# An adapter with layer norm over 128 batches: h in pairs, b1 from TensorE, language numbers loaded two at a time

## The chip, the cores and the metric

One core of a Trainium2 chip runs the whole program. The metric is the device time of one execution in microseconds (us). PE is TensorE, PEld its weight loads, DVE is VectorE, ACT is ScalarE, POOL is GpSimd and SP the queue that issues most DMAs. A q behind a name (PEldq, ACTq) marks what the engine's sequencer does itself: register loads, branches, DMA issues.

## The reference

For each of 128 batches, with x[b] of 128 rows by 512 and a language number lang in 0 to 9:

```python
h = relu(x[b] @ W1[lang] + b1[lang])          # 128 x 128
y = x[b] + h @ W2[lang] + b2[lang]            # 128 x 512
n = (y - mean(y)) / sqrt(var(y) + 1e-5)
out[b] = x[b] + n * gamma[lang] + beta[lang]
```

## The kernel before

Batches go through in order, 16 to a turn: turn 0 is unrolled, turns 1 to 6 are one hardware loop (`all_turns`), and turn 7 is unrolled. Each engine has its own program, and semaphores that count batches tie them together. x lies in 16 slots of `x_io`; SP moves it in pairs of batches (512 KB), stores a pair once it is finished, and one pair later loads that slot with the x of the next turn (`store_pair`, `load_pair`, L217 to L226).

For batch t the work goes as follows.
- PE turns x by four transposes (`turn_x`, L385) into a bank `ps_T`. ACT copies it to `x_T` (L323).
- PE multiplies by W1 in full fp32 (`first_product`, L392: four products, shown as eight weight loads and matmuls) into `ps_h`. ACT copies h to `h_rows` (L328), PE turns it (`turn_h`, L400), and ACT applies relu with b1 as its per-partition bias, twice: into `h_high`, a rounded fp32r (L337), and into `h_T`, fp32 (L338). The bias is picked by a language number in a register of ACT. POOL subtracts the two to get `h_low` (L263).
- PE forms y in one of four banks `ps_y` (`second_product`): b2 by a bf16 product with `pick` and `parts` (L409), then h_high by w2_high (L411), h_high by w2_low (L412), h_low by w2_high (L414). For slots 1, 5, 9 and 13 there is no L409: POOL adds b2 to x (L279), and `x_b2` takes the place of x.
- DVE adds x and takes the row sum (`add_x`, L501), ACT squares (L343), DVE takes the mean of a pair (L506), ACT the root of a pair (L348), DVE the reciprocal (L511), then y minus mean times gamma (`scale`, L518) and the end result into the slot of x (`finish`, L526). POOL adds beta to x for it (L272).

In PE's program step j of a turn holds turn_h(t-1), turn_x(t+1), first_product(t) and second_product(t-3). A second product waits until its bank is free, that is until `finish` of four batches earlier. DVE runs norms four batches behind.

Language numbers stand in `lang_ids` and are needed in registers. At the start of each turn PE, ACT, POOL and DVE each load those of the whole turn and of the batches that lag behind, with one TENSOR_LOAD in the trace (`langs_of`, L139): 20 values on PE, 16 on ACT, 20 on POOL and 16 on DVE in a turn of the loop. Behind the last turn PE and ACT load one, POOL two and DVE four.

Ahead of turn 0, gamma and beta are spread over the partitions by PE (L452, from `parts`, which SP fills with three bf16 pieces of each row), and DVE cuts w2 into high and low parts in five chunks (L488, L490), from a buffer `w2_all` of its own. PE does first products of batches 0 to 4 meanwhile and then waits for the last chunk (L436). SP's order there is x pair 0, w1, `parts`, x pair 1, w2 with x pairs 2 and 3 in between, x pairs 4 to 7, and b2 for all partitions (L215).

Of the kernel before, what the change touches and what calls it, by code (L numbers as in the profile page):

```python
# [13 lines left out]
UNROLL = 16  # L14
PAIRS = UNROLL // 2
Y_BANKS = 4
LAG = 4
H_SLOTS = 8
H_T_SLOTS = 4
B2_BY_POOL = (1, 5, 9, 13)  # L20
B2_LATE = 2
NORM_LAG = 4


def build(nc, x, ids, w1, b1, w2, b2, gamma, beta, out):
# [3 lines left out]
    TURNS = B // UNROLL  # L29
    W_CHUNKS = 5  # L30
    LC = L // W_CHUNKS
    X_AFTER_W2 = (1, 4)
    assert S == 128 and A == 128 and H == 512 and B % UNROLL == 0 and TURNS > 2

# [4 lines left out]
    with ExitStack() as ctx:  # L39
# [9 lines left out]

        w1_all = sb("w1_all", [128, L, C, A], F32)  # L50
        w2_all = sb("w2_all", [128, L, H], F32)
# [6 lines left out]
        b1_all = sb("b1_all", [128, L], F32)  # L58

# [4 lines left out]
        parts = sb("parts", [128, H], BF16)  # L64
        pick_row = sb("pick_row", [128, 3 * L], BF16)
# [6 lines left out]

        x_io = sb("x_io", [128, UNROLL, H], F32)
        x_T = sb("x_T", [128, 2, C, S], F32)
        h_rows = sb("h_rows", [128, 2, A], F32)
        h_T = sb("h_T", [128, H_T_SLOTS, S], F32)
        h_high = sb("h_high", [128, H_SLOTS, S], F32R)
        h_low = sb("h_low", [128, H_SLOTS, S], F32R)
        squares = cut
        row_sum = sb("row_sum", [128, UNROLL], F32)  # L80
        mean = sb("mean", [128, UNROLL], F32)
        sq_sum = sb("sq_sum", [128, UNROLL], F32)
        table_load = sb("table_load", [128, 1], F32)
        std = sb("std", [128, UNROLL], F32)
        rstd = sb("rstd", [128, UNROLL], F32)
# [7 lines left out]
        s_b1 = sem("s_b1")  # L93
        s_rows = sem("s_rows")
        s_b2 = sem("s_b2")
        x_b2_ready = sem("x_b2_ready")
# [11 lines left out]
        pick_ready = sem("pick_ready")  # L108
        cut_step = sem("cut_step")
        parts_ready = sem("parts_ready")  # L110
# [4 lines left out]
        x_beta_ready = sem("x_beta_ready")  # L115
        x_turned = sem("x_turned")
        x_T_ready = sem("x_T_ready")
        h_summed = sem("h_summed")
# [5 lines left out]
        adapted = sem("adapted")  # L124
        y_ready = sem("y_ready")
        squared = sem("squared")
        scaled = sem("scaled")
        out_ready = sem("out_ready")

# [7 lines left out]
        def langs_of(engine, t, n):  # L137

            return nc.values_load_multi_w_load_instructions(  # L139
                lang_ids[0:1, bass.ds(t, n)], engines=[engine.engine], min_val=0, max_val=L - 1,  # L140
                skip_runtime_bounds_check_because="VectorE keeps lang_ids within the tables")[1]

        def seconds_done(j, first, last):

            if j < 0:
                return 0 if first else j - LAG + 1
            if first:
                return max(0, j - LAG + 1)
            if last:
                return min(j, j - LAG + 1 + (j + 1) // (UNROLL // (LAG - 1)))  # L150
            return j - LAG + 1

        def seconds(j, first, last):

            return range(seconds_done(j - 1, first, last), seconds_done(j, first, last))

        LEFT = B - seconds_done(UNROLL - 1, False, True) - (TURNS - 1) * UNROLL
        LEFT_NORMS = B - seconds_done(UNROLL - 2, False, True) - (TURNS - 1) * UNROLL

# [3 lines left out]
        def b2_by_pool(j, first):  # L163
            return j in B2_BY_POOL[B2_LATE if first else 0:]

# [3 lines left out]
        def b2_count(i, j):  # L169

            return i * len(B2_BY_POOL) + B2_BY_POOL.index(j) + 1 - B2_LATE

        def w2_chunk(table, n):
            return table[:, n * LC:(n + 1) * LC, :]

# [4 lines left out]

# [6 lines left out]
        def _(sp):  # L187
            sp.dma_start(ids_raw[:, :], ids.rearrange("(a b) -> a b", a=1)).then_inc(s_ids, 16)
            for k, table in enumerate((b2, gamma, beta)):
                sp.dma_start(rows[k * L:(k + 1) * L, :], table).then_inc(s_rows, 16)  # L190
            def first_x(k):
                sp.dma_start(x_io[:, 2 * k:2 * k + 2, :], x_pairs[:, k, :, :]).then_inc(x_loaded[k], 16)

            def load_w2(n):
                sp.dma_start(w2_chunk(w2_all, n), w2[n * LC:(n + 1) * LC].rearrange("l a h -> a l h"))\
# [13 lines left out]
            for n in range(W_CHUNKS):  # L209
                load_w2(n)  # L210
                if n in X_AFTER_W2:
                    first_x(2 + X_AFTER_W2.index(n))
            for k in range(2 + len(X_AFTER_W2), PAIRS):
                first_x(k)
            sp.dma_start(b2_all[:, :, :], b2.partition_broadcast(128)).then_inc(s_b2, 16)  # L215

            def store_pair(i, k):  # L217
                sp.wait_ge(out_ready, i * UNROLL + 2 * k + 2)
# [9 lines left out]

            def turn(i, first, last):
                for k in range(PAIRS):  # L230
                    if last and k == PAIRS - 1:
                        for b in range(2):
                            sp.wait_ge(out_ready, B - 1 + b)
                            sp.dma_start(out[B - 2 + b], x_io[:, UNROLL - 2 + b, :]).then_inc(stored[k], 16)
# [12 lines left out]
        def _(pool):  # L247
            nc.gpsimd.memset(parts[:, :], 0.0).then_inc(parts_zero, 1)
            nc.gpsimd.memset(identity[:, :], 0.0).then_inc(set_ready, 1)
# [9 lines left out]
            def low_h(t, j):  # L259
                pool.wait_ge(h_high_ready, t + 1)  # L260
                pool.wait_ge(h_T_ready, t + 1)

                nc.gpsimd.tensor_tensor(h_low[:, j % H_SLOTS, :], h_T[:, j % H_T_SLOTS, :],  # L263
                                        h_high[:, j % H_SLOTS, :].bitcast(F32), ALU.subtract).then_inc(h_low_ready, 1)

            pool.wait_ge(ids_ready, 1)
            pool.wait_ge(spread_act, L)
# [314 lines left out]
```

## Time and profile before

| | |
|---|---|
| median of 3 runs | 377.81 us (376.56 to 378.6) |
| profiled execution, span | 373.9 us |
| PE busy | 317.1 us (85%) |
| DVE busy | 314.1 us (84%) |
| ACT busy | 284.8 us (76%) |
| POOL busy | 257.4 us (69%) |
| mean granted TensorE clock | 0.972 |
| DMA over the span | 202 GB/s |

The profiled execution is one of its own; the profile gives its span, from the first to the last instruction, as its only time, and the median of the timed runs lies 3.9 us above that. Busy shares are averages over stages. Ends of matmuls are modelled, so that the distance between starts of consecutive matmuls tells their cost, not the duration beside them. Some matmul records are missing.

### The profile page before, as it was taken

The page shows a single profiled execution, that of the slowest core. Times are in us where ns is not written, and L with a number is a line of the kernel's source. Part 1 is how long each engine was busy: PE and PEld are TensorE (multiplying, and loading weights), DVE is VectorE, ACT ScalarE, POOL GpSimd, SP SyncE. Part 2 cuts the span into 40 slices and gives each one's busy share as a digit, 9 for nine tenths or more (in the row PEclk, how much of TensorE's full clock was granted, in tenths as well). Part 3 has the DMA queues.
Part 4 walks back from the last instruction along what each step waited for, and adds up shares of the span by engine and source line. Part 5 has one row for each costly group of instructions (what it writes and reads, how often), then busy time and mean ns, then how long its engine had stood idle before and what let it go on. Part 6 is the DMA issues. An engine that isn't in the chain of part 4 may idle for free. (4 is left out here: it accounts for less than half of the span.)

```text
span 373.9 us, 9114 instructions
## 1 busy us (share of the span) xinstructions
PE 317.1 (85%) x2133; PEld 274.5 (73%) x2167; DVE 314.1 (84%) x669; ACT 284.8 (76%) x848; POOL 257.4 (69%) x299
## 2 busy tenths in 40 slices
PE   1888996999878996899879997989969999879870
PEld 0277985889767995789768895879858897767850
DVE  3695995799869995699957997699957998799997
ACT  5666994799687995789858895979947996967871
POOL 2034784688677884788847885878846886767882
PEclk9999998999999999899989999999989999999996
DMA  7999365376744666366634766447653666556333
GB/s 179 320 387 419 118 222 175 113 236 228 231 148 173 224 224 224 112 203 240 218 125 168 234 227 224 156 155 232 227 172 112 231 224 229 178 183 213 124 122 130
DMA packets 43047, 75.35 MB, mean 202 GB/s; under 512 B 3612, under 2 KB 8823, under 8 KB 42901
## 3 DMA queue, kind: packets, MB, share of 16 engines
q1 hardware_dynamic: 41733, 75.14, 58.8%
q10 hardware_dynamic: 1296, 0.01, 0.2%
q8 instruction: 8, 0.13, 0.2%
q14 instruction: 10, 0.08, 0.1%
HBM read 41.49 MB, written 33.55 MB: 201 GB/s over the span
## 5 line engine op out<-in xcount | busy, mean ns | idle before, releaser
L272 POOL TENSOR_TENSOR x_io<-x_io,beta_all 128x512 f32<-128x512 f32 x128 | 163.7, 1279 | 15.1 <-DVE ps_y L501 13.8
L392 PE MATMUL ps_h<-w_all,x_T 128*128 x1024 | 138.0, 278 | 0.4 <-ACT x_T L323 0.4
L392 PEld LDWEIGHTS ps_h<-w_all,x_T 128*128 128x128 f32 x1024 | 126.8, 195 | 0.8 <-issue 0.7
L263 POOL TENSOR_TENSOR h_low<-h_T,h_high 128x128 fp32r<-128x128 f32 x128 | 60.3, 471 | 94.5 <-ACT h_T L338 87.2
L343 ACT ACTIVATE cut<-ps_y,row_sum 128x512 bf16<-128x512 f32 x128 | 88.8, 694 | 15.7 <-DVE ps_y L501 15.7
L526 DVE SCALAR_TENSOR_TENSOR x_io<-ps_y,rstd,x_io 128x512 f32<-128x512 f32 x128 | 94.6, 739 | 0.0
L518 DVE SCALAR_TENSOR_TENSOR ps_y<-ps_y,mean,gamma_all 128x512 f32<-128x512 f32 x128 | 89.6, 744 | 0.7
L501 DVE SCALAR_TENSOR_TENSOR ps_y<-ps_y,x_io 128x512 f32<-128x512 f32 x98 | 67.4, 688 | 20.4 <-PE ps_y L414 20.4
L385 PE MATMUL ps_T<-identity,x_io 128*128 128x128 f32 x512 | 78.7, 277 | 6.1 <-DMA x_io<-in_x 6.1
L337 ACT ACTIVATE h_high<-ps_hT,b_all 128x128 fp32r<-128x128 f32 x128 | 46.2, 361 | 44.9 <-PE ps_y L414 29.6
L411 PE MATMUL ps_y<-w_high,h_high 128*128 x128 | 71.3, 557 | 7.7 <-DVE x_io L526 4.6
L323 ACT COPY x_T<-ps_T 128x512 f32<-128x512 f32 x128 | 74.8, 585 | 0.0
L385 PEld LDWEIGHTS ps_T<-identity,x_io 128*128 128x128 f32 x512 | 61.3, 143 | 15.0 <-issue 6.6
L400 PE MATMUL ps_hT<-identity,h_rows 128*128 128x128 f32 x128 | 36.4, 284 | 21.7 <-ACT h_rows L328 14.4
L412 PE MATMUL ps_y<-w_low,h_high 128*128 x128 | 51.6, 403 | 0.0
L414 PE MATMUL ps_y<-w_high,h_low 128*128 x128 | 51.4, 402 | 0.0
L338 ACT ACTIVATE h_T<-ps_hT,b_all 128x128 f32<-128x128 f32 x128 | 46.0, 359 | 0.0
L400 PEld LDWEIGHTS ps_hT<-identity,h_rows 128*128 128x128 f32 x128 | 18.2, 142 | 35.5 <-ACT h_rows L328 19.5
L328 ACT COPY h_rows<-ps_h 128x128 f32<-128x128 f32 x128 | 34.3, 268 | 12.7 <-PE ps_h L392 3.1
L506 DVE TENSOR_SCALAR mean<-row_sum 128x2 f32<-128x2 f32 x64 | 42.9, 670 | 0.0
L279 POOL TENSOR_TENSOR x_b<-x_io,b_all 128x512 f32<-128x512 f32 x30 | 38.5, 1285 | 0.0
L409 PE MATMUL ps_y<-parts,pick 128*128 128x512 bf16 x65 | 24.7, 380 | 8.1 <-DVE x_io L526 7.9
(43 smaller groups left out, 219.5 us busy)
## 6 DMA issues: line engine op xcount, KB each, us to landing
x_io<-in_x SPq DMA_DIRECT2D x64, 512.0 KB, 4.1
out<-x_io SPq DMA_DIRECT2D x63, 512.0 KB, 3.0
w_all<-in_L_cond_W SPq DMA_DIRECT2D x10, 512.0 KB, 6.8
b_all<-in_L_cond_b SPq DMA_DIRECT2D x1, 2560.0 KB, 17.2
out<-x_io SPq DMA_DIRECT2D x2, 256.0 KB, 2.0
parts<-cut SPq DMA_DIRECT2D x3, 30.0 KB, 3.6
rows<-in_L_cond_b SPq DMA_DIRECT2D x1, 20.0 KB
rows<-in_L_cond_gamma SPq DMA_DIRECT2D x1, 20.0 KB
```

The costliest lines, as they stand in the source:

```text
L263: nc.gpsimd.tensor_tensor(h_low[:, j % H_SLOTS, :], h_T[:, j % H_T_SLOTS, :], h_high[:, j % H_SLOTS, :].bitcast(F32), ALU.subtract).then_i ...
L272: nc.gpsimd.tensor_tensor(x_io[:, j, :], x_io[:, j, :], of_lang(beta_all, lang), ALU.add)\
L323: nc.scalar.copy(x_T[:, j % 2, :, :], ps_T[j % 2][:, :, :]).then_inc(x_T_ready, 1)
L343: nc.scalar.activation(squares[:, j % 2, :], ps_y[j % Y_BANKS][:, :], ACT.Square, scale=-float(H), bias=row_sum[:, j:j + 1], accum_out=sq_ ...
L385: last = nc.tensor.transpose(ps_T[j % 2][:, c, :], x_io[:, j, c * 128:(c + 1) * 128], identity[:, :])
L392: last = nc.tensor.matmul(ps_h[:, 0:A], x_T[:, j % 2, c, :], w1_all[:, bass.ds(lang, 1), c, :].rearrange("p o a -> p (o a)"), start=(c == ...
L400: nc.tensor.transpose(ps_hT[:, 0:S], h_rows[:, j % 2, :], identity[:, :]).then_inc(h_turned, 1)
L411: nc.tensor.matmul(bank, h_high[:, h, :], of_lang(w2_high, lang), start=not with_b2, stop=False)
L412: nc.tensor.matmul(bank, h_high[:, h, :], of_lang(w2_low, lang), start=False, stop=False)
L501: nc.vector.scalar_tensor_tensor(bank, bank, 1.0, x_rows, ALU.mult, ALU.add, accum_out=row_sum[:, j:j + 1]).then_inc(y_ready, 1)
L518: nc.vector.scalar_tensor_tensor(bank, bank, mean[:, j:j + 1], of_lang(gamma_all, lang), ALU.subtract, ALU.mult).then_inc(scaled, 1)
L526: nc.vector.scalar_tensor_tensor(x_io[:, j, :], ps_y[j % Y_BANKS][:, :], rstd[:, j:j + 1], x_io[:, j, :], ALU.mult, ALU.add).then_inc(out_ ...
```

## The change

- **Pairs.** h is handled by pairs of batches: both first products write halves of the one bank `ps_h`, one ACT instruction of 256 columns copies both, both are turned into halves of `ps_hT`, and each split (high, T, low) is one instruction of 256 columns. Steps on every engine are pairs; 64 steps take the place of 128.
- **b1 by PE.** `first_product` begins with a bf16 product of `pick` and `b1_parts` (128 columns). relu moves to the copy of h ahead of the turn. ACT needs no language number any more. `b1_parts` is made as `parts` is: a load on ACT's queue, three casts and two subtractions on DVE, three DMAs on SP ahead of those of `parts`, one more memset on POOL.
- **Languages by two.** `langs_of` loads two values: PE twice in each step (for its first and its second products), DVE once, POOL once, and once more in the steps with an add of b2.
- **Order.** PE's step k: turn_x of pair k+1 and first products of pair k, interleaved; second products of pair k-2; turn_h of pair k. DVE's step: scales of pair k-3, adds of pair k-2, reciprocal and finishes of pair k-3. ACT's: the two copies of x_T interleaved with the two squares of pair k-3, copy of h, mean and root, then the split of h. POOL's: low part of pair k-1, beta for pair k-3, b2 for pair k-2 where it has one. The last step does two second pairs.
- **Mean on ACT**, after the copy of h, in place of L506 on DVE.
- **w2 staged in x_io.** `w2_all` is gone; the five chunks land in the slots of x pairs 3 to 7, and those pairs are loaded one by one when `w2_low_ready` tells that the chunk is cut. b2 for all partitions is issued behind them.
- POOL's adds of b2 are now those of slots 4, 7, 10 and 13.

```diff
-UNROLL = 16
-LAG = 4
-B2_BY_POOL = (1, 5, 9, 13)
-NORM_LAG = 4
+SLOTS = 16
+LAG = 2
+NORM_LAG = LAG + 1
+H_PAIRS = 4
+B2_BY_POOL = (4, 7, 10, 13)
...
-        def langs_of(engine, t, n):
+        def langs_of(engine, t):
             return nc.values_load_multi_w_load_instructions(
-                lang_ids[0:1, bass.ds(t, n)], ...
+                lang_ids[0:1, bass.ds(t, 2)], ...
...
# SP
                 if n == 1:
-                    sp.wait_ge(parts_zero, 1)
+                    sp.wait_ge(parts_zero, 2)
+                    for k in range(3):
+                        sp.wait_ge(b1_cut_step, 2 * k + 1)
+                        sp.dma_start(b1_parts[32 * k:32 * k + L, :], b1_cut[:, k, :]).then_inc(b1_parts_ready, 16)
...
-                if n in X_AFTER_W2:
-                    first_x(2 + X_AFTER_W2.index(n))
-            for k in range(2 + len(X_AFTER_W2), PAIRS):
-                first_x(k)
+                if n == 1:
+                    first_x(2)
+            for n in range(W_CHUNKS):
+                sp.wait_ge(w2_low_ready, n + 1)
+                first_x(X_FIRST + n)
...
# POOL
+            def step(i, k, has_low, has_sum, has_norm, first):
+                if has_norm:
+                    langs = langs_of(pool, t - 2 * NORM_LAG)
+                if has_low:
+                    low_h(p - 1, (k - 1) % PAIRS)
+                if has_norm:
+                    for b in range(2):
+                        add_beta(t - 2 * NORM_LAG + b, (2 * (k - NORM_LAG) + b) % SLOTS, langs[b])
+                if has_sum:
+                    for b in range(2):
+                        j = (2 * (k - LAG) + b) % SLOTS
+                        if b2_by_pool(j, in_first):
+                            add_b2(t - 2 * LAG + b, j, langs_of(pool, t - 2 * LAG)[b], first)
...
# ACT
+            def copy_h(p, k):
+                act.wait_ge(h_summed, p + 1)
+                nc.scalar.activation(h_rows[:, k % 2, :, :].rearrange("p b a -> p (b a)"), ps_h[:, 0:2 * A], ACT.Relu)\
+                    .then_inc(h_rows_ready, 1)
+            def split_h(p, k, fresh):
+                act.wait_ge(h_turned, p + 1)
+                if not (fresh and k < H_PAIRS):
+                    act.wait_ge(adapted, 2 * (p - H_PAIRS) + 2)
+                if not (fresh and k < 2):
+                    act.wait_ge(h_low_ready, p - 1)
+                nc.scalar.copy(h_high[...], ps_hT[:, 0:2 * S]).then_inc(h_high_ready, 1)
+                nc.scalar.copy(h_T[...], ps_hT[:, 0:2 * S]).then_inc(h_T_ready, 1)
...
+            def mean_and_root(t, j):
+                nc.scalar.mul(mean[:, j:j + 2], row_sum[:, j:j + 2], 1.0 / H).then_inc(mean_ready, 1)
+                act.wait_ge(squared, t + 2)
+                nc.scalar.activation(std[:, j:j + 2], sq_sum[:, j:j + 2], ACT.Sqrt, ...).then_inc(std_ready, 1)
+            def step(i, k, has_x, has_h, has_norm, first):
+                for b in range(2):
+                    if has_x:
+                        act.wait_ge(x_turned, t + 3 + b)
+                        nc.scalar.copy(x_T[:, j % 4, :, :], ps_T[j % 2][:, :, :]).then_inc(x_T_ready, 1)
+                    if has_norm:
+                        square(u + b, v + b)
+                if has_h:
+                    copy_h(p, k)
+                if has_norm:
+                    mean_and_root(u, v)
+                if has_h:
+                    split_h(p, k, first)
...
# PE
+            def first_product(j, lang):
+                part = ps_h[:, (j % 2) * A:(j % 2 + 1) * A]
+                nc.tensor.matmul(part, of_lang(pick, lang), b1_parts[:, :], start=True, stop=False)
+                for c in range(C):
+                    last = nc.tensor.matmul(part, x_T[:, j % 4, c, :], ..., start=False, stop=(c == C - 1))
+                if j % 2 == 1:
+                    last.then_inc(h_summed, 1)
...
             def turn(i, first, last):
+                for k in range(PAIRS):
+                    langs = langs_of(pe, t)
+                    for b in range(2):
+                        pe.wait_ge(x_T_ready, t + b + 1)
+                        if not (last and k == PAIRS - 1):
+                            turn_x(i + (k + 1) // PAIRS, (2 * k + 2 + b) % SLOTS)
+                        first_product(2 * k + b, langs[b])
...
+                    for q in seconds(k, last):
+                        if not (first and q < 0):
+                            second_pair(i, q, first and 2 * q < Y_BANKS, first)
+                    turn_h(p, k)
...
# DVE
+            def step(i, k, sums, late_sums, has_norm, first):
+                if has_norm:
+                    langs = langs_of(dve, u)
+                    for b in range(2):
+                        scale(u + b, q, j + b, langs[b])
+                for s in sums:
+                    add_pair(i, s, first)
+                if has_norm:
+                    invert(q, j)
+                    for b in range(2):
+                        finish(u + b, q, j + b)
+                for s in late_sums:
+                    add_pair(i, s, first)
```

`second_pair` loads its two languages first, then is `second_product` for each batch of the pair, with the waits for `h_high` and `h_low` once a pair.

## Rows read from the trace of the kernel before

**Rows 1.** One line (L182), PE's branch at each loop end: times in ns, first and last.

```profile
L182 PEldq COMPARE_BRANCH  x6: 83/215/242, 97.7 to 312.7; - x6
```

**Rows 2.** Timeline of PE across a turn's end: start, us, what, [idle before].

```profile
134.78 0.40 PE L414 MATMUL ps_y<-w_high,h_low 128*128 x1
...
136.93 0.40 PE L414 MATMUL ps_y<-w_high,h_low 128*128 x1
...
139.29 0.39 PE L414 MATMUL ps_y<-w_high,h_low 128*128 x1
...
139.63 0.60 PE L385 MATMUL ps_T<-identity,x_io 128*128 128x128 f32 x4
140.06 1.06 PE L392 MATMUL ps_h<-w_all,x_T 128*128 x8
140.96 0.38 PE L409 MATMUL ps_y<-parts,pick 128*128 128x512 bf16 x1
...
143.09 0.32 PE L400 MATMUL ps_hT<-identity,h_rows 128*128 128x128 f32 x1 [1.05 <-issue]
...
147.69 0.33 PE L400 MATMUL ps_hT<-identity,h_rows 128*128 128x128 f32 x1 [2.03 <-ACT h_rows L328]
```

**Rows 3.** Waits by pair of lines: us in total, times, longest.

```profile
ACT h_high L337 <- PE ps_y L414: 29.6, 7, 4.4
```

**Rows 4.** Timeline of ACT in the same stretch.

```profile
146.37 0.37 ACT L337 ACTIVATE h_high<-ps_hT,b_all 128x128 fp32r<-128x128 f32 x1 [4.27 <-PE ps_y L414]
...
146.88 0.58 ACT L323 COPY x_T<-ps_T 128x512 f32<-128x512 f32 x1
147.35 0.29 ACT L328 COPY h_rows<-ps_h 128x128 f32<-128x128 f32 x1
147.51 0.72 ACT L343 ACTIVATE cut<-ps_y,row_sum 128x512 bf16<-128x512 f32 x1
```

**Rows 5.** One line (L139), the language loads: ns min/median/max, first and last start.

```profile
L139 ACTq TENSOR_LOAD <-lang_ids x9: 281/4657/4733, 2.9 to 362.9; - x9
L139 PEldq TENSOR_LOAD <-lang_ids x9: 310/2362/2504, 6.2 to 361.9; - x9
L139 POOLq TENSOR_LOAD <-lang_ids x9: 819/5857/6273, 19.2 to 364.1; - x9
L139 DVEq TENSOR_LOAD <-lang_ids x9: 350/1626/2226, 27.9 to 362.6; - x9
```

**Rows 6.** Instructions grouped by line: mean ns of one, idle time before them.

```profile
L506 DVE TENSOR_SCALAR mean<-row_sum 128x2 f32<-128x2 f32 x64 | 42.9, 670 | 0.0
...
L409 PEld LDWEIGHTS ps_y<-parts,pick 128*128 x98 | 9.7, 99 | 17.8 <-issue 17.7
```

**Rows 7.** Timeline of DVE in the same stretch.

```profile
140.66 1.39 DVE L518 SCALAR_TENSOR_TENSOR ps_y<-ps_y,mean,gamma_all 128x512 f32<-128x512 f32 x2
141.97 0.73 DVE L526 SCALAR_TENSOR_TENSOR x_io<-ps_y,rstd,x_io 128x512 f32<-128x512 f32 x1
142.62 0.68 DVE L501 SCALAR_TENSOR_TENSOR ps_y<-ps_y,x_io 128x512 f32<-128x512 f32 x1
```

**Rows 8.** Timeline of POOL: the same stretch, then the end.

```profile
139.98 1.28 POOL L272 TENSOR_TENSOR x_io<-x_io,beta_all 128x512 f32<-128x512 f32 x1
141.21 0.47 POOL L263 TENSOR_TENSOR h_low<-h_T,h_high 128x128 fp32r<-128x128 f32 x1
...
365.11 1.27 POOL L272 TENSOR_TENSOR x_io<-x_io,beta_all 128x512 f32<-128x512 f32 x1 [0.52 <-issue]
```

**Rows 9.** Timeline of the start: the first second product.

```profile
29.65 0.49 PE L411 MATMUL ps_y<-w_high,h_high 128*128 x1 [2.33 <-DVE w_low L490]
```

**Rows 10.** One line (L224), SP's loads of x.

```profile
DMA to landing us min/median/max: 3.7/4.1/5.4
```

**Rows 11.** Timeline of the end: the last L414 and the last finishes.

```profile
364.64 0.50 PE L414 MATMUL ps_y<-w_high,h_low 128*128 x1
...
369.89 1.41 DVE L526 SCALAR_TENSOR_TENSOR x_io<-ps_y,rstd,x_io 128x512 f32<-128x512 f32 x2
```

More of the change, by code:

```diff
@@ L373, in _ @@
+            for j in range(2):
+                act.wait_ge(x_turned, j + 1)
+                nc.scalar.copy(x_T[:, j, :, :], ps_T[j][:, :, :]).then_inc(x_T_ready, 1)
+            def turn(i, first, last):
+                for k in range(PAIRS):
+                    step(i, k, not (last and k == PAIRS - 1), True, not (first and k < NORM_LAG), first)
             all_turns(act, turn)
-            relu(B - 1, UNROLL - 1, langs_of(act, B - 1, 1)[0], False)
-            for k in range(LEFT_NORMS, 0, -1):
-                norm_sums(B - k, UNROLL - k)
+            for k in range(NORM_LAG):
+                step(TURNS, k, False, False, True, False)
@@ L419, in turn @@
-            def turn(i, first, last):
-                behind = 0 if first else LAG
-                langs = first_langs if first else langs_of(pe, i * UNROLL - behind, UNROLL + behind)
-                for j in range(UNROLL):
-                    t = i * UNROLL + j
-                    early = first and j <= LAG
-                    if not early:
-                        turn_h(t - 1, (j - 1) % UNROLL)
-                    if not (last and j == UNROLL - 1):
-                        turn_x(t + 1, i + (j + 1) // UNROLL, (j + 1) % UNROLL)
-                    if early and j > 0:
-                        turn_h(t - 1, (j - 1) % UNROLL)
-                    first_product(t, j, langs[j + behind])
-                    if first and j == LAG:
+                                            start=False, stop=(c == C - 1))
@@ L547, in step @@
-                if has_sum:
-                    add_x(t - 1, i + (j - 1) // UNROLL, (j - 1) % UNROLL, early)
-            def turn(i, first, last):
-                behind = 0 if first else NORM_LAG
-                langs = langs_of(dve, i * UNROLL - behind, UNROLL - NORM_LAG + behind)
-                for j in range(UNROLL):
-                    has_norm = not (first and j < NORM_LAG)
-                    step(i, j, langs[j - NORM_LAG + behind:] if has_norm else None, has_norm,
-                         not (first and j < 2), not (first and j == 0), first)
+                    langs = langs_of(dve, u)
@@ new lines, in step @@
+                    for b in range(2):
+                        scale(u + b, q, j + b, langs[b])
[3 more added lines that the diff above has]
+                    invert(q, j)
+                    for b in range(2):
+                        finish(u + b, q, j + b)
+                for s in late_sums:
+                    add_pair(i, s, first)
+            def turn(i, first, last):
+                for k in range(PAIRS):
+                    sums = [q for q in seconds(k, last) if not (first and q < 0)]
+                    step(i, k, sums[:1], sums[1:], not (first and k < NORM_LAG), first)
```

304 lines of the change are left out of this document (124 added, 180 removed).

## The prediction, made before the change was run

> **What bounds the kernel now.** I read busy shares first: PE and DVE both near 85%, which says little. So I measured a turn. PE's loop branch comes six times from 97.7 to 312.7 us, so a turn of 16 batches takes 43.0 us [rows 1], 5.38 a pair. The timeline of PE then shows what a batch costs when nothing waits: starts of L414 are 2.15 us apart without L409 and 2.36 with it [rows 2]; twelve batches in sixteen have it, so the mean is 2.31 and a turn of pure PE work 36.9. Inside a turn PE sets the pace; 6.1 us a turn are lost at its end. There PE waits 1.05 us for nothing that shows and 2.03 for h_rows [rows 2], ACT stands 4.27 us before L337 [rows 4], and so it is seven times, 29.6 us in all [rows 3]. The releaser named there, L414, had long been done: what holds ACT is its language load, 16 values in 4.66 us, while PE loads 20 in 2.36 and POOL 20 in 5.86 [rows 5]. The start up to 29.65 us [rows 9] and the end behind the last L414 at 364.64 [rows 11] are no steady work.
>
> **Language loads.** ACT's go altogether, and with them the chain that makes the turn's end expensive: up to 6.1 us a turn, 7 turns' ends, 43 us. In their place PE loads two values twice in a step. One value took PE 310 ns and twenty 2362 [rows 5]: 0.2 plus 0.108 a value, so two are 0.42 us. Such a load stalls PE only by what PE's queue has not covered. At the turn's end a load of 2.36 left 1.05 of idle PE [rows 2, 5], so 1.3 us of matmuls were queued ahead. I take the 0.42 as hidden, under the first products for the one and, for the one at the step's start, under second products queued before; this needs h_rows early, as worked out below. Bounds: 0 and 0.84 us a step. On DVE four values took 0.35 [rows 5]; I charge 0.25 a step, partly covered by the finish before it. On POOL two take 0.82, of which 0.52 showed as idle [rows 5, 8].
> The Trainium skill (Perfetto Trace Analysis, Sequencer Loop) says that a sequencer pushes engine instructions into a queue and runs control work itself. Only row 5 beside row 2 prices that here; the trace agrees in kind, with 1.3 us of cover.
>
> **PE.** b1 adds 128 bf16 products of 128 columns. No row has one. From below, a quarter of the 0.21 that L409's 512 columns add [rows 2] is 0.05; from above, a bf16 weight load is 0.10 [rows 6] and the moving side may not hide it. The neighbours are short too, one f32 transpose each 0.11 (four in 0.43 [rows 2]), so I take the upper end, 0.10. Batch 2.41, pair 4.82 us. The rest of PE's work is the same matmuls.
> TensorE: Matmul & The Clock Gate (the Trainium skill, Back-to-back issue gap) gives about 81 ns for a sustained load and matmul of 128 columns. By that the pair is 4.78 and the end 2.4 us earlier. The rows with 0.10 are nearer to this sequence.
>
> **ACT.** From starts: copy of x_T 0.47, square with its accumulator read 0.75 (the row has 0.72 for the square alone), copy of h 0.16 [rows 4]. From 128 to 512 columns a copy grows from 0.16 to 0.47, so 0.10 for each 128: copy of a pair 0.27, each split 0.36. Mean and root are small, 0.2 each. Sum 0.94 + 1.5 + 0.27 + 0.4 + 0.72 = 3.8 a step: not the bound.
>
> **DVE.** Two scales 1.31, one finish 0.65 [rows 7]; an add about the same. Six of them and a reciprocal: 4.0, with the load 4.25. L506 goes (0.67 each [rows 6]; for two numbers in a row that is mostly waiting); I book no gain, because DVE inside a turn waited for PE.
>
> **POOL.** low_h of 256 columns: 0.47 at 128, 1.28 at 512 [rows 8], so 0.74. Two betas at 1.23 from start to start, 2.46. Half an add of b2, 0.6. With loads of 0.5 each, 1.5 of them: 4.6 a step on average, but 5.4 in a step with b2.
>
> **The loops.** Three engines near 4.8 need their handoffs checked. Count from the end of PE's turn_h. ACT: handoff 0.3, split 0.72, copy 0.47, square 0.75, copy 0.47, square 0.75, copy of h 0.27, mean 0.3: DVE's scales start at 4.0, and the copy of h is there by 3.8, before PE wants it at 4.6. DVE: two scales, two adds, reciprocal, first finish end at 4.0 + 1.3 + 1.3 + 0.1 + 0.7 = 7.4; PE wants that bank in its next step at 4.82 + 2.86 = 7.7. Slack 0.3. The shorter loop, from scales to the next scales: 1.3, first add and handoff 0.75, then on ACT 0.75 + 0.47 + 0.75 + 0.27 + 0.3 = 4.6. Slack 0.2. POOL's b2: low_h starts at 1.2 and ends at 1.9, betas to 4.4, then up to 0.5 of load and 1.23: ready 5.6 to 6.2, and DVE's adds come at 5.3 (slots 4, 10) or 6.0 (7, 13). Late by 0 to 0.9 in four steps of a turn, part of it taken by the slack: I take 1.0 a turn, 0.13 a step. Step 4.95 us.
>
> **Ahead of the loop.** PE's second products began at 29.65, released by the last w2 chunk on DVE [rows 9]. The b1 path adds five small DVE instructions, which run while the rows for L472 are still coming, and three DMAs of SP ahead of those of `parts`. Each lands in some us but they overlap; the delay of `parts` is their issue, 0 to 1.5 us, I take 0.6. The memset on POOL is hidden by the same wait. Slots of x 3 to 7 wait for their chunks, some 2 us apart, the last near 30: landing takes 4.1, at most 5.4 [rows 10], and pair 7 is turned four steps later. Not on the path, and b2 behind it on SP's queue is first wanted some five steps on. The first products of three pairs fit before 30.3, as those of five batches did before 29.65. Later in the kernel, by the loop times above, pair k is finished 3.3 us into step k+4; SP loads its slot behind the store of pair k+1, 3.3 + 0.4 into step k+5, and the x lands 4.1 later, 3.0 into step k+6. PE turns it from the start of step k+7: slack 1.8 us, and 0.5 with a landing of 5.4. Free.
>
> **Sum.** 30.3; rest of that step (second pair 1.75, turn_h 0.22) 2.0; 61 steps of 4.95, 302; the extra second pair of the last step 1.75. DVE then has its late pair of adds (1.3, from 1.3 after PE's step), the norms of three pairs at 2.8 and one more pair of adds (1.3): 12.4 in all. 348.4, and 2.6 from the end of DVE (369.89 + 1.41 = 371.3 [rows 11]) to the end of the span, 373.9: span 351.0. The median lies 3.9 above the profiled span before; with that 354.9, so **355**.
>
> **Rivals.**
> 1. *Loads exposed on PE, slower than before.* Every step PE's queue is empty when a load starts, because it had just waited for h_rows or for a bank. Then 0.84 a step come on top: 61 x 0.84 = 51, 406 us; only one of two exposed gives 381. It decides from a step of 5.32 on (355 + 61 x 0.37 = 377.8). Against it: 1.3 us of cover [rows 2, 5] and h_rows 0.8 early. For it: all engines have 0.2 to 0.3 of slack, and a queue that waits is an empty one. Chance 0.11.
> 2. *The loops bind.* Each handoff 0.1 longer over four of them, or POOL late at each b2: step 5.15 to 5.3, 367 to 376. Chance 0.22.
> 3. *PE alone binds.* b1 at 0.05 to 0.10, POOL's lateness absorbed: step 4.72 to 4.82, 341 to 347. Chance 0.2.
> 4. *The turn's end stays.* If its 6.1 us are the branch or fetched code and not loads, 355 + 7 x 6 = 397. Against it: PE has the idle also where an unrolled turn begins without a branch, seven waits for six branches [rows 1, 3]. Chance 0.03.
> The forecast itself, step 4.87 to 5.1, has 0.44.
>
> **The numbers.** The range 341 to 377 holds rivals 2 and 3 and the forecast; 1 and 4 stay outside. A measurement of this kernel tells about 0.5% from no change. Faster by more: forecast, 2, 3, most of it: 0.85. Same: 0.04. Slower: 0.11, from 1 and 4.
>
> **What would show it.** A turn of 8 steps in about 39.6 us (43.0 before); L337's waits of 4 us gone; the granted clock at its upper level through the loop; PE with at most 0.2 us of idle a step; waits of DVE for x_b in steps of slots 4 and 10. Wrong: PE idle "issue" before first transposes or L409 in each step (rival 1), h_rows or finish as PE's releaser above 0.3 us a step (rival 2), gaps each 40 us (rival 4).

## The result and the profile after

The median of the changed kernel is 391.13 us (four runs, 389.4 to 393.35), that of the kernel before in the same session 377.69 (376.56 to 378.6). The ratio is 1.035 with a 95% interval of 1.031 to 1.040: the change made the kernel 3.5% slower. 355 was predicted, in a range of 341 to 377, and the slower side had 0.11. The profiled execution has a span of 391.3 us; 351.0 was worked out for it.

First the page of the changed kernel, its busy shares:

```profile
span 391.3 us, 9509 instructions
...
PE 333.6 (85%) x2294; PEld 279.3 (71%) x2295; DVE 287.6 (73%) x610; ACT 249.7 (64%) x719; POOL 244.4 (62%) x236
```

PE's share is what it was, DVE's fell from near 85% to 73%. So no engine took PE's place as the bound, and PE itself has holes. PE's branch at the loop's end (now L173), the counterpart of [rows 1], dates the turns:

```profile
L173 PEldq COMPARE_BRANCH  x6: 83/218/249, 101.0 to 319.8; - x6
```

A turn takes 43.8 us where it took 43.0. The first branch comes 3.3 us later than before, the last 7.1 later, and from there to the end of the span it is 71.5 us instead of 61.2. So the 17.4 us of difference between the two spans are 3.3 ahead of the first branch, 3.8 over five turns and 10.3 behind the last branch. The turn should have fallen to 39.6, and its end was indeed repaired: no wait of ACT for an L414 is left in the list of waits. What stands in its place (us in total, times, longest):

```profile
DVE ps_y L512 <- ACT mean L340: 75.5, 60, 3.1
PEld ps_T L381 <- issue: 43.1, 58, 5.5
...
PE ps_T L381 <- issue: 24.2, 54, 0.8
PE ps_y L411 <- DVE x_io L524: 12.0, 2, 8.6
...
DVE ps_y L500 <- POOL x_b L272: 7.3, 3, 6.1
```

The line to read is the third: 54 times, before the first transpose of a step, PE stands still and no semaphore holds it. (PEld is PE's weight load; its line is the same wait.) DVE's wait in the first line is DVE being early: in the fastest version below it is still 49.2 us in 60 waits. The timeline of PE shows two ends of steps in the unrolled turn 0 and two in the loop (start, us, what, idle before):

```profile
38.30 0.38 PE L397 MATMUL ps_hT<-identity,h_rows 128*128 128x128 f32 x2
38.52 0.60 PE L381 MATMUL ps_T<-identity,x_io 128*128 128x128 f32 x4
...
43.24 0.38 PE L397 MATMUL ps_hT<-identity,h_rows 128*128 128x128 f32 x2
...
156.51 0.38 PE L397 MATMUL ps_hT<-identity,h_rows 128*128 128x128 f32 x2
157.33 0.63 PE L381 MATMUL ps_T<-identity,x_io 128*128 128x128 f32 x4 [0.44 <-issue]
...
162.09 0.38 PE L397 MATMUL ps_hT<-identity,h_rows 128*128 128x128 f32 x2
```

From one turn_h to the next it is 4.94 us in turn 0, and there the transposes follow 0.22 behind it. In the loop it is 5.58, and they follow 0.82 behind it. From turn_h at 33.37 to turn_h at 358.49 lie 60 steps, so the mean is 5.42. What PE runs at that point between the two is its language load (L139; ns min/median/max of all, then single loads in two narrow stretches):

```profile
L139 PEldq TENSOR_LOAD <-lang_ids x128: 531/552/1639, 17.9 to 367.4; - x128
L139 POOLq TENSOR_LOAD <-lang_ids x94: 503/512/727, 28.1 to 376.2; - x94
L139 DVEq TENSOR_LOAD <-lang_ids x64: 523/528/784, 33.6 to 384.6; - x64
...
L139 PEldq TENSOR_LOAD <-lang_ids x1: 1522/1522/1522, 155.6 to 155.6; - x1
...
L139 PEldq TENSOR_LOAD <-lang_ids x1: 550/550/550, 158.8 to 158.8; - x1
```

The median says 0.55 us and hides the matter. 56 of the 128 loads take over 0.9 us (0.93 to 1.64, 50 of them 1.2 or more), and all 56 are loads at the start of a step; those in the middle of a step are all short. The load of 155.6 ends at 157.1, 0.3 before the transpose that comes late. And SP's queue at that time:

```profile
154.55 0.38 SPq L215 DMA_DIRECT2D out<-x_io  x1
155.12 0.39 SPq L220 DMA_DIRECT2D x_io<-in_x  x1
160.00 0.38 SPq L215 DMA_DIRECT2D out<-x_io  x1
160.57 0.39 SPq L220 DMA_DIRECT2D x_io<-in_x  x1
```

SP issues a store and a load of x each step, and the second issue ends at 155.5, where PE's long load begins. Each of the 56 long loads begins between 0.3 us ahead of and 0.7 us behind the end of an issue of SP. That is a coincidence until a run moves one of the two. It is also no rule: nine loads, of the start, of turn 0 and of the end, begin as close to an issue and take 0.53 to 0.83 us.

The end of the kernel (PE, then POOL and DVE):

```profile
358.49 0.38 PE L397 MATMUL ps_hT<-identity,h_rows 128*128 128x128 f32 x2
...
366.59 0.60 PE L411 MATMUL ps_y<-parts,pick 128*128 128x512 bf16 x1 [3.42 <-DVE x_io L524]
...
369.55 0.45 PE L397 MATMUL ps_hT<-identity,h_rows 128*128 128x128 f32 x2
...
373.95 1.26 POOL L272 TENSOR_TENSOR x_b<-x_io,b_all 128x512 f32<-128x512 f32 x1
375.33 0.70 DVE L500 SCALAR_TENSOR_TENSOR ps_y<-ps_y,x_b 128x512 f32<-128x512 f32 x1 [6.06 <-POOL x_b L272]
...
387.34 1.41 DVE L524 SCALAR_TENSOR_TENSOR x_io<-ps_y,rstd,x_io 128x512 f32<-128x512 f32 x2
```

The last step has two second pairs, and the later one needs a bank that DVE must finish first: 3.42 us of idle PE ahead of it, and only behind it comes the last turn_h. On that ACT and POOL's low_h depend; POOL's betas and x_b stand behind low_h in its program, and for x_b DVE waits 6.06 us. From turn_h of 358.49 to the end of the span it is 32.6 us (counted from its end at 358.7); the sum had 21.7. After the idle stretches the granted clock falls too: 1.00 through the loop, 0.57 from 366 us on, mostly the lower level of 1.2 GHz.

### The profile page after: what moved, and what is told of

It reads as the page before. It is cut to its first block and busy times, and to the rows that moved or that the text cites. A ratio compares the mean times of both kernels' runs of the same rounds, so it can differ in the third digit from the quotient of the medians.

```text
span 391.3 us, 9509 instructions
## 1 busy us (share of the span) xinstructions
PE 333.6 (85%) x2294; PEld 279.3 (71%) x2295; DVE 287.6 (73%) x610; ACT 249.7 (64%) x719; POOL 244.4 (62%) x236
## 5 line engine op out<-in xcount | busy, mean ns | idle before, releaser
L388 PE MATMUL ps_h<-w_all,x_T 128*128 x1024 | 142.0, 282 | 0.0
L259 POOL TENSOR_TENSOR h_low<-h_T,h_high 128x256 fp32r<-128x256 f32 x64 | 46.8, 731 | 134.5 <-ACT h_T L331 134.5
L524 DVE SCALAR_TENSOR_TENSOR x_io<-ps_y,rstd,x_io 128x512 f32<-128x512 f32 x128 | 90.2, 746 | 2.6
L329 ACT CAST h_high<-ps_hT 128x256 fp32r<-128x256 f32 x64 | 23.9, 373 | 86.5 <-PE ps_hT L397 86.5
L414 PE MATMUL ps_y<-w_high,h_high 128*128 x128 | 71.4, 558 | 0.1
L415 PE MATMUL ps_y<-w_low,h_high 128*128 x128 | 51.6, 404 | 0.0
L418 PE MATMUL ps_y<-w_high,h_low 128*128 x128 | 51.3, 401 | 0.0
L411 PE MATMUL ps_y<-parts,pick 128*128 128x512 bf16 x98 | 38.4, 391 | 12.1 <-DVE x_io L524 12.0
L272 POOL TENSOR_TENSOR x_b<-x_io,b_all 128x512 f32<-128x512 f32 x30 | 38.6, 1287 | 0.0
L418 PEld LDWEIGHTS ps_y<-w_high,h_low 128*128 128x128 f32 x128 | 24.6, 192 | 5.9
L411 PEld LDWEIGHTS ps_y<-parts,pick 128*128 x98 | 9.6, 98 | 26.6 <-issue 26.6
L386 PE MATMUL ps_h<-b_parts,pick 128*128 128x128 bf16 x128 | 28.0, 219 | 0.1
L415 PEld LDWEIGHTS ps_y<-w_low,h_high 128*128 128x128 f32 x128 | 24.9, 195 | 3.2
L500 DVE SCALAR_TENSOR_TENSOR ps_y<-ps_y,x_b 128x512 f32<-128x512 f32 x30 | 21.3, 710 | 7.4 <-POOL x_b L272 7.3
```

The lines of the kernel that those rows point to most:

```text
L388: last = nc.tensor.matmul(part, x_T[:, j % 4, c, :], w1_all[:, bass.ds(lang, 1), c, :].rearrange("p o a -> p (o a)"), start=False, stop=(c ...
L411: nc.tensor.matmul(bank, of_lang(pick, langs[b]), parts[:, :], start=True, stop=False)
L414: nc.tensor.matmul(bank, h_high[:, h, b, :], of_lang(w2_high, langs[b]), start=not with_b2, stop=False)
L415: nc.tensor.matmul(bank, h_high[:, h, b, :], of_lang(w2_low, langs[b]), start=False, stop=False)
L418: nc.tensor.matmul(bank, h_low[:, h, b, :], of_lang(w2_high, langs[b]), start=False, stop=True)\
L500: nc.vector.scalar_tensor_tensor(bank, bank, 1.0, x_rows, ALU.mult, ALU.add, accum_out=row_sum[:, j:j + 1]).then_inc(y_ready, 1)
```

## The experiments

The theory after reading: the load at a step's start is exposed on PE, since it stands where PE's sequencer has just waited for h_rows; and it is so long because SP issues DMAs at that moment. Rivals: the loops through ACT, DVE and POOL bind, so that PE's idle time is only where their wait shows (rival 2); the new matmul is what costs.

### The load taken ahead of the second products

```diff
-                    langs = langs_of(pe, t)
+                    langs = langs_of(pe, t) if k == 0 else next_langs
...
+                    if k < PAIRS - 1:
+                        next_langs = langs_of(pe, t + 2)
                     for q in seconds(k, last):
```

> After the change, with the language load at the start of PE's steps 1 to 7 of a turn moved ahead of the second products of the step before (two loads stand there together; step 0 of each turn keeps its load at the start). Theory (the load at the step's start is what holds PE: it takes 1.2 to 1.6 us where the other takes 0.54, and PE idles about 0.6 us a step for it): 52 of 60 steps lose 0.5 to 0.6 us, so 391 goes to 360 to 366, steps without the load at 4.8 to 4.95 as in turn 0. Rival (the loops over DVE and ACT set 5.4 us a step, and the load only fills a gap that is there anyway): 389 to 392, with DVE or ACT named as what PE waits for. Second rival (any load behind another is slow too, so that it is late for b2's product): about 375.

370.56 us, ratio 0.984 to the kernel before (0.979 to 0.989). That is 20.6 less than the changed kernel by the medians, and 23.1 by the spans of the profiled executions (368.2 and 391.3). PE's branches and loads:

```profile
L173 PEldq COMPARE_BRANCH  x6: 76/210/246, 98.2 to 300.8; - x6
...
L139 PEldq TENSOR_LOAD <-lang_ids x128: 530/547/1743, 18.0 to 345.0; - x128
```

A turn takes 40.5 us. There are as many loads as before the edit, and they are short but for seven, those of the steps k = 0, whose load was left in place. In the loop these steps take 6.2 to 6.5 us, more than the 5.4 to 5.7 that they took in the changed kernel (5.8 as the loop is entered, 5.1 in turn 7). The others have this timeline:

```profile
120.32 0.38 PE L397 MATMUL ps_hT<-identity,h_rows 128*128 128x128 f32 x2
125.04 0.38 PE L397 MATMUL ps_hT<-identity,h_rows 128*128 128x128 f32 x2
130.12 0.38 PE L397 MATMUL ps_hT<-identity,h_rows 128*128 128x128 f32 x2
```

4.72 and 5.08 us. The first is twice 2.46 (2.36 of [rows 2] with 0.10 for b1) less one L411 (0.21 by [rows 2]): pure PE work as it was costed. So the loops don't bind at 5.4, and rival 2 as the explanation of the loss is out. The time was 4.6 us over the upper end of what was expected: the steps k = 0, which grew, and the steps of 5.08 with POOL's b2 were not in it.

### The last step in another order

```diff
-                    for q in seconds(k, last):
+                    for n, q in enumerate(seconds(k, last)):
...
-                    turn_h(p, k)
+                        if n == 0:
+                            turn_h(p, k)
```

Beside it POOL adds its last two b2 ahead of the last low_h and betas, not behind them.

> After the change, two orders at the very end: the last step's turn_h stands between its two second pairs on PE, and POOL adds b2 for the last pair that has one ahead of the last low part. Theory (11 us of the excess over the prediction are made there: PE waits 3.4 us for a bank ahead of turn_h, POOL's add comes 6 us late and DVE waits for it): 7 to 10 us less, 381 to 384. Rival (DVE's backlog of three pairs of norms sets the end in any order): at most 2 us less, 389 to 391.

385.57 us, ratio 1.025 (1.019 to 1.030): 5.6 us less than the changed kernel, where 7 to 10 were expected. By the profiled executions the stretch from the last turn_h but one to the end of the span fell from 32.6 to 26.3 us, so 6.3 of the 10.9 by which the end was missed were its order; the mean step, 5.39 for 5.42, gave some 2 us more there. Which of the two orders, PE's or POOL's, is worth what was not taken apart.

### SP's DMAs moved, PE's loads left in place

```diff
-                sp.wait_ge(out_ready, i * SLOTS + 2 * k + 2)
+                if isinstance(i, int) and i == TURNS - 1 and k > 3:
+                    sp.wait_ge(out_ready, i * SLOTS + 2 * k + 2)
+                else:
+                    sp.wait_ge(h_turned, i * PAIRS + k + 5)
```

The store of a pair, and with it the load of x behind it, waits until PE has done the turn_h of four pairs later, in place of the finish. That turn_h comes behind the finish in any case, since the second products ahead of it need the bank.

> After the change, SP's stores wait for PE's turn_h of four pairs later (which lies about 1.5 us behind the finish they waited for) instead of for the finish itself; PE's program is untouched. Theory (a language load that runs into SP's issue of a DMA is held until about 1.5 us after that issue; the load at the step's start is the one that does): that load falls to 0.54 us and its idle goes, and the load in the middle may become the long one, where PE has cover: 358 to 370. Rival (the load at a step's start is long because turn_h stands ahead of it in PE's queue, or because DVE's scales run): it stays at 1.2 to 1.6 us, and the time at 391 or above, up to 400 if x now lands late.

375.22 us, ratio 0.997 (0.994 to 0.999), span 373.3. SP's queue, then single loads of PE, then PE:

```profile
152.65 0.38 SPq L218 DMA_DIRECT2D out<-x_io  x1
153.22 0.39 SPq L223 DMA_DIRECT2D x_io<-in_x  x1
...
L139 PEldq TENSOR_LOAD <-lang_ids x1: 551/551/551, 151.1 to 151.1; - x1
...
L139 PEldq TENSOR_LOAD <-lang_ids x1: 1540/1540/1540, 153.7 to 153.7; - x1
...
152.10 0.38 PE L400 MATMUL ps_hT<-identity,h_rows 128*128 128x128 f32 x2
152.32 0.60 PE L384 MATMUL ps_T<-identity,x_io 128*128 128x128 f32 x4
```

This is the run that decides. No load of PE was touched, yet the one at the step's start is now 0.55 us, at every step, and in the lines shown the transposes follow 0.22 behind turn_h. The load in the middle of the step, which SP's issue now meets, has become the long one, 54 times. There it costs little, as first products are queued ahead. The length belongs to the meeting with what SP issues, not to the place in PE's program. (Issue and transfer moved together, so this run can't tell them apart.) The time fell 16 us but not into the expected range, because a new wait came in, x arriving late:

```profile
PE ps_T L384 <- DMA x_io<-in_x: 16.4, 19, 5.9
```

### b1 on TensorE alone

The kernel before, with the b1 product ahead of each first product, the relu at the copy of h, plain copies for the split, and so no load on ACT; single batches, loads once a turn, mean on DVE.

```diff
+                nc.tensor.matmul(ps_h[:, 0:A], of_lang(pick, lang), b1_parts[:, :], start=True, stop=False)
...
-                langs = first_langs if first else langs_of(act, i * UNROLL - behind, UNROLL - 1 + behind)
```

> The kernel before, with only b1 moved to PE (relu at the copy of h, no language load on ACT); batches one by one, languages a turn at a time on PE, POOL and DVE. It costs 128 products of 0.10 us, 13 us, and takes ACT's load of 4.66 us out of each turn's end. Theory (ACT's load was what held the turn's end): of 6.1 us a turn some 4 go, 7 x 4 = 28 less, 377.8 + 13 - 28 = 363, with PE's own 1.05 and a part of POOL's left. Rival (POOL's load of 5.86 takes its place at once, low_h being queued behind it): 1 us a turn, 377.8 + 13 - 7 = 384. Second rival (the end of the turn is not loads): 391.

367.54 us, ratio 0.977 (0.971 to 0.982). PE at two turns' ends:

```profile
60.25 0.32 PE L403 MATMUL ps_hT<-identity,h_rows 128*128 128x128 f32 x1 [0.31 <-issue]
...
101.97 0.32 PE L403 MATMUL ps_hT<-identity,h_rows 128*128 128x128 f32 x1 [1.37 <-issue]
```

The turn is 41.7 us. Inside it a batch is 2.41 on average, 38.6 for sixteen, so the turn's end loses 3.1 where it lost 6.1. This part of the change alone is worth 2.3%: it confirms that ACT's language load made about half of what the turn's end lost in [rows 3, 4], and that pairs, small loads and the mean on ACT were not needed for that gain. It came out 4.5 us above the 363 expected, and well below the rivals' 384 and 391.

### Both repairs, then step 0

Loads early and the new end together:

> e1 and e2 together: loads ahead of the second products, and the two orders at the end. Theory (the two losses have nothing to do with each other): 370.6 - 5.5 = 365, steps of 4.94, 4.72 and 5.07 as in e1, with about 6.2 in step 0 of a turn. Rival (with shorter steps DVE's backlog covers the end): 368 to 370.

364.91 us, ratio 0.966 (0.961 to 0.971), as expected; the two gains, 20.6 and 5.6, add up (391.13 less 26.2 is 364.9). To a tenth that is luck: these runs stand in different sessions, in which the median of the kernel before lay between 376.3 and 378.4. In this kernel a step k = 0 has idle PE at its start:

```profile
140.75 0.66 PE L386 MATMUL ps_T<-identity,x_io 128*128 128x128 f32 x4 [1.17 <-issue]
```

So both pairs of transposes were put ahead of the load there:

```diff
-                    langs = langs_of(pe, t) if k == 0 else next_langs
+                    if k == 0:
+                        for b in range(2):
+                            pe.wait_ge(x_T_ready, t + b + 1)
+                            turn_x(i, 2 + b)
+                        langs = langs_of(pe, t)
+                    else:
+                        langs = next_langs
...
+                        if k > 0 and not (last and k == PAIRS - 1):
```

> e5, and in step 0 of each turn PE turns both batches of x, which needs no language, ahead of the load that still stands there. Theory (that load takes 1.2 to 1.5 us because SP issues DMAs then; step 0 costs 1.2 us over the others, and 0.86 us of transposes now run under it): step 0 at 5.1 to 5.6, 7 x 0.86 = 6 less, 359. Rival (both banks are then turned before ACT has copied, or x_T comes late, and the first products wait): 365, the idle standing before L388.

363.48 us, ratio 0.963 (0.958 to 0.968), 1.4 less, where about 6 was expected. PE at such a step's start:

```profile
139.42 1.04 PE L386 MATMUL ps_T<-identity,x_io 128*128 128x128 f32 x8
140.66 0.23 PE L391 MATMUL ps_h<-b_parts,pick 128*128 128x128 bf16 x1 [0.21 <-issue]
...
143.43 0.39 PE L416 MATMUL ps_y<-parts,pick 128*128 128x512 bf16 x1 [0.48 <-DVE x_io L539]
```

The idle time did go, from 1.17 to 0.21 us, and the step fell only from 6.2 to 5.95. The last line shows where the rest went. L416 could follow the first products at 142.8 and starts 0.6 us later. The finish that is named had ended at 142.5; what ended last are PE's two loads of 0.53 and 0.54 us, of 141.9 and 142.6, one right behind the other. In the other steps the same two begin 1.2 us behind turn_h and are covered; here they begin 2.7 behind it, since the sequencer had been held by the load of step 0. With 0.4 ahead of L391 that is the 1.0 us that step 0 has over 4.94 (its own work is 4.72, as its pair has one b2 from POOL, so strictly it loses 1.2). In turn 7, which no taken branch precedes, the load of step 0 begins 0.5 us earlier against turn_h and the step takes 5.12; as the loop is entered, also without a taken branch, it takes 5.74. So a part of the turn's end seems to be the loop's own, on PE's sequencer; no run took that out.

### b1 left out, on the version with both repairs

```diff
-                nc.tensor.matmul(part, of_lang(pick, lang), b1_parts[:, :], start=True, stop=False)
...
-                                            start=False, stop=(c == C - 1))
+                                            start=(c == 0), stop=(c == C - 1))
```

> e5 without the product of b1; b1 is left out of the computation. Theory (PE sets every step, and b1 costs 0.10 us a batch): step 4.72 to 4.74 with b2 twice instead of 4.94, 128 x 0.10 = 13 less, 352. Rival (other engines stand right behind PE, as the loops of the prediction said): DVE and ACT hold the step at 4.8 to 4.9, 357 to 361.

358.15 us, ratio 0.948 (0.944 to 0.953), 6.8 less, where the theory had 13 and the rival 4 to 8. The product removes 128 x 0.10 = 12.8 us of PE's work; where nothing else held, the steps fell from 4.94 to 4.73, 0.2 for two products, the price of the prediction. But the mean step went from 5.04 to 4.92 only. So the loops stand right behind PE, some 0.1 us away by this, and there is little left for PE to give.

### PE's loads once a turn again

The changed kernel, with PE alone loading 20 values at a turn's start:

```diff
-                    langs = langs_of(pe, t)
+                    langs = turn_langs[2 * k + behind:]
```

> After the change, with PE's languages alone loaded a turn at a time again (20 values); POOL and DVE still load two. Theory (the change's loss is the load at each step's start on PE): 60 times 0.6 goes, and 7 turns' ends cost 1 to 3 us each, 391 - 36 + 14 = 369, between 362 and 373. Rival (loads on POOL and DVE matter as well): 380 or more.

373.76 us, ratio 0.991 (0.988 to 0.994), 17.4 less than the changed kernel. The loads:

```profile
L139 PEldq TENSOR_LOAD <-lang_ids x9: 550/2347/2596, 17.9 to 348.4; - x9
```

Seven steps in eight are 4.72 to 5.01, step 0 is 6.8 to 7.06 in the loop (6.4 in turn 7), some 2 us more, of which 1.0 is left in the version of step 0 too. That is cheaper than eight exposed loads that lose 0.47 each, and dearer than loads that are covered (370.56 in the first experiment).

### The mean back on DVE, on the version of step 0

```diff
-                nc.scalar.mul(mean[:, j:j + 2], row_sum[:, j:j + 2], 1.0 / H).then_inc(mean_ready, 1)
...
+                    dve.wait_ge(y_ready, u + 2)
+                    nc.vector.tensor_scalar(mean[:, j:j + 2], row_sum[:, j:j + 2], 1.0 / H, None, ALU.mult)\
+                        .then_inc(mean_ready, 1)
```

> e6 with the mean back on DVE, ahead of the scales, which then wait for the squares alone. Theory (PE sets the step; DVE waits 0.76 us a step for ACT's mean with time to spare, 45.8 us in 60 waits): 363.5, within 1; the wait is renamed, not gone, since ACT's second square ends 0.3 us ahead of its mean. Rival (ACT's mean stands in the loop that holds step 0 and the steps with x_b): 359 to 361. Rival on the other side (the small operation costs DVE 0.3 to 0.6 a step, as L506 seemed to before): 366 to 370.

369.78 us, ratio 0.979 (0.975 to 0.983), 6.3 more: not the 363.5 of the theory, but the second rival. DVE's timeline:

```profile
102.34 1.41 DVE L538 SCALAR_TENSOR_TENSOR x_io<-ps_y,rstd,x_io 128x512 f32<-128x512 f32 x2
103.67 0.66 DVE L549 TENSOR_SCALAR mean<-row_sum 128x2 f32<-128x2 f32 x1
104.56 1.42 DVE L526 SCALAR_TENSOR_TENSOR ps_y<-ps_y,mean,gamma_all 128x512 f32<-128x512 f32 x2 [0.23 <-DVE mean L549]
```

From the start of the mean to that of the scales it is 0.89 us for two numbers a row. The mean of the steps goes from 5.01 to 5.09 us. In the loop it is two steps in eight that grow, from 4.94 and 4.72 to about 5.18 and 4.95, and in turns 1 and 7 most of them (up to 5.4). That makes 4.8 of the 6.3 us; 1.6 more lie behind the last turn_h but one. So there DVE is in a loop that binds.

### Other slots for POOL's b2

```diff
-B2_BY_POOL = (4, 7, 10, 13)
+B2_BY_POOL = (3, 7, 11, 15)
```

> e6 with POOL's adds of b2 at slots 3, 7, 11 and 15: always the second batch of a pair, in every other pair. Theory (POOL's add comes late for the first batch of a pair, step 5.08 where 4.72 is PE's work; DVE waits 5.7 us for x_b in all): three or four waits fewer a turn, all steps 4.72 or 4.94 apart from step 0, 2 to 3 us less, 361. Rival (only PE's work moves about): 363.5, within 0.5.

360.51 us, ratio 0.954 (0.950 to 0.958): as expected, and the best that computes everything; it is 4.6% faster than the kernel before and 7.8% faster than the changed one (360.51 to 391.13, both against the same kernel before within 0.2%). Its page and PE's turn_h:

```profile
span 358.8 us, 9488 instructions
...
PE 325.5 (91%) x2294; PEld 282.6 (79%) x2295; DVE 287.3 (80%) x610; ACT 241.1 (67%) x719; POOL 245.1 (68%) x236
...
114.82 0.38 PE L402 MATMUL ps_hT<-identity,h_rows 128*128 128x128 f32 x2
...
119.52 0.38 PE L402 MATMUL ps_hT<-identity,h_rows 128*128 128x128 f32 x2
...
124.47 0.38 PE L402 MATMUL ps_hT<-identity,h_rows 128*128 128x128 f32 x2
```

One b2 by POOL falls into every other step, always the second batch of its pair, so it has time, and the step it falls into saves PE one L416: 4.70 and 4.95 in turn. The waits of DVE for POOL's x_b, first of the version of step 0, then of this one:

```profile
DVE ps_y L515 <- POOL x_b L272: 5.7, 15, 1.1
```

```profile
DVE ps_y L515 <- POOL x_b L272: 0.5, 1, 0.5
```

## Why the prediction was wrong

The experiments are called e1 to e10, in the order of the labels above.

**The step that failed** is the sentence "I take the 0.42 as hidden". It fails by the size; the cover was smaller too, though it would have done for 0.42.
- The size. 0.42 was worked out from loads of one and of twenty values [rows 5]. A load of two takes 0.55 on PE when it stands alone, and mostly 1.2 to 1.6 where SP issues a store and a load of x. The numbers of [rows 5] could not show that. e3, with SP's DMAs moved, shows that the length follows SP's issue.
- The cover. 1.3 us of matmuls queued ahead was read at a turn's end. At a step's start the load begins at 155.6 and turn_h at 156.51, so 0.9 us of second products are ahead, and with turn_h itself 1.1. The trace says why the sequencer comes there no earlier. It is turn_h's wait for h_rows, ACT's copy of h, which ends at 155.4:

```profile
155.02 0.38 ACT L320 ACTIVATE h_rows<-ps_h 128x256 f32<-128x256 f32 x1
```

Of the 56 long loads 40 begin 0.15 us behind the end of this copy and 7 begin 0.05 behind it, whatever else the step does. So h_rows, though 0.9 to 1.1 us early for turn_h itself, as the prediction had it, sets how much is queued. The 1.1 are enough for 0.55, as turn 0 and e3 show, and 0.4 short of 1.5; the transposes then start 0.3 behind the load's end. The prediction had its own warning in rival 1: "a queue that waits is an empty one".

It was rival 1 that came, in its weaker form, one load of two exposed. It was priced at 0.42 a step and 381 us; the 60 steps from turn_h to turn_h cost 0.47 each over the forecast, 28.1 of the 40.3 us between the two spans. e1 gives back 23.4 of the 28.1; the other 4.7 stand in the steps k = 0, where the load was left (6.0 us each on average). The bound of 0.84 a step held this, but the time had been kept out of the range by a chance that took the load's duration as known. A duration that is interpolated between two far rows deserves a wide price, and here the range should have reached 381.

**The end.** The sum had 12.4 us from the last step to DVE's end and 21.7 from turn_h of the step before to the end of the span; it was 32.6. It left out that the last step's later second pair waits for a bank that DVE finishes (3.42 us) while turn_h stands behind it, and that POOL's last x_b is queued behind the last low_h and betas. e2 gives 6.3 of the 10.9 back by the spans. Behind those pauses the clock is at the lower level for a time, and L415 to L418 takes 0.43 us there in place of 0.23; its part in the rest no run took apart.

**The start.** The step of pair 2 ended at 33.6 (turn_h at 33.37) where 32.3 was worked out, +1.3; 1.06 us of idle PE is one wait for x at 28.33, for the first of the pairs whose slots had staged w2. Such slots were thus nearly, not wholly, free.

**From the span to the median.** The prediction added 3.9, the distance between the median and the profiled span before. The executions listed lie 1.7 to 2.1 us above their own spans, but for one of 2.8; the rest of the 3.9 was then the profiled execution being a fast one. For the changed kernel it was the slowest of four, and the distance is -0.2. This took 4.1 off. So 28.1 + 10.9 + 1.3 - 4.1 is 36.2, the 36.1 between 391.1 and 355.

**What held.** PE's work of 4.94 a step, 4.72 with one b2 less: turn 0, e1 and e10 show both to a few hundredths (against 4.95 in the forecast, of which 4.82 was PE). b1 at 0.10 a product: e7. The turn's end as the work of ACT's load, in part: e4 takes it from 6.1 to 3.1 us, and the wait for L414 vanished. POOL late with b2: the wait list has it in e6, and e10 takes it away, 3.0 us of the 8 predicted (0.13 a step). That the loops stand close behind PE: slack of 0.2 to 0.3 was worked out, and in e7 they bind once PE has about 0.1 less. Rival 4 has a part: of the 1.0 us over 4.94 that e6 leaves in step 0 of the loop's turns, 0.2 is left in turn 7, which no taken branch precedes.

**"I book no gain" for the mean** was too low. On the repaired version the move to ACT is worth 6.3 us (e9), since with the mean DVE is in a loop that binds in some steps. In the changed kernel PE's idle time, presumably, stood in front of it.

The Trainium skill (TensorE: Matmul & The Clock Gate, Back-to-back issue gap) gives about 81 ns for a weight load and product of 128 columns. By that, as an estimate, b1 costs 10.4 us in all; e7's steps give 0.10 each, 12.8 us, and the measurement decides.

One sum of the prediction is slightly off, without effect: 355 + 61 x 0.37 is 377.6, not 377.8.

## What to carry to other kernels

A value loaded into an engine's registers costs what the work queued ahead of it doesn't cover, so its place counts as much as its size: put the load where matmuls or other work are queued ahead of it, never right behind a wait, and look at what the DMA-issuing engine does at that moment, because here most loads grew two to three times when they met. Read single durations, not the median, for anything repeated: here a median of 552 ns hid 56 loads of 0.93 to 1.64 us. And draw the last step of a pipelined loop by itself: the order that is right in the steady state puts the longest chain last.

## What was not expected of the hardware

- A load of two values into registers takes 0.55 us on PE, 0.53 on DVE and 0.51 on POOL, and twenty 2.35 on PE. When PE's began near the end of SP's issues of a store and a load of x (512 KB each), it took 0.93 to 1.64 us and ended 1.0 to 1.6 us behind the second issue. On POOL and DVE the longest of all was 0.73 and 0.79. The changed kernel's own trace narrows down which of the two does it. In turn 7 two loads began 0.7 and 0.3 us behind the issue of a store with no load of x behind it and took 1.23 (at 352.3) and 1.35 us (357.4): a store seems to be enough. At 22.6, 26.8 and 30.8 PE's load met the issue of a load of x alone and took 0.55 each time. But it isn't the store in every case: at 362.2 a load begins with the end of a store's issue and takes 0.55. By what path, and whether the descriptors or the moving data count, stays open.
- Before, four values on DVE took 0.35 [rows 5]; two take 0.53 now. Why is open.
- The mean on DVE, two numbers a row, occupies 0.69 us at the median of e9 (0.16 to 1.07), and in the lines shown it is 0.89 from its start to that of the scale that uses it: as much as a pass over 512 columns (0.65 by [rows 7]). It isn't the size: the reciprocal of the same two numbers takes 0.16 each time in that kernel too. The mean on ACT takes 0.21. Why it is so long on DVE is open.
